# The centre tap of the FFN's convolution, made by GpSimd instead of ScalarE

## The chip, the cores and the metric

One core of one Trainium2 chip runs the whole program in one launch. The metric is the device time of a launch in microseconds. The kernel before takes 1537.39 us, the median of 3 runs (1535.62 to 1537.73).

The core's engines work side by side, each through its own queue in program order, and wait for each other on semaphores: TensorE (PE in the profile; its weight loads are PEld), VectorE (DVE), ScalarE (ACT), GpSimd (POOL), and SyncE (SP), which here issues the DMAs.

## The reference

`x` is [64, 128, 256], `ctx` is [64, 128, 192], all float32. Everything is per sequence of 128 tokens.

```python
# cross attention, 16 heads of 64; the last 4 context tokens have weights and a softmax of their own
xn  = layernorm(x)
q   = xn @ Wq + xn @ q_down @ q_up * (q_alpha / 32)
k,v = the same from ctx[:, :124] with Wk, Wv;   k2,v2 = ctx[:, 124:] @ Wk_ipa, @ Wv_ipa
o   = softmax(q k^T / 8) v + softmax(q k2^T / 8) v2
x   = x + o @ Wo + bo + o @ o_down @ o_up * (o_alpha / 32)
# FFN with quantised activations and ternary weights
h   = quant(layernorm(x)) @ ternary(w1).T                     # [64, 128, 1024]
h   = conv_w[:,0]*h[t-1] + conv_w[:,1]*h[t] + conv_w[:,2]*h[t+1] + conv_b   # per channel, along the tokens
h   = silu(h)
x   = x + quant(h) @ ternary(w2).T
```

The change is in the term `conv_w[:,1]*h[t] + conv_b`, the centre tap.

## The kernel before

**Groups and half-steps.** The 64 sequences are 16 groups of four (`GROUPS`, `NB`). A group is worked in 32 half-steps, n = 0 to 31 (`HALVES`), two to a step; a step is one chunk of attention (one sequence, four heads). Each engine has a function `steps(g, n)` that issues, for half-step n, its part of attention for group g, of the projections for group g+1, and of the FFN (`finish`) for group g-1, whose own half-steps run from 0 to 44 and so reach into g-2's place. `run_groups` (L134) writes this out for groups 0, 1, the last and the two drains, and has a hardware loop for groups 2 to 14. So attention of one group, the projections of the next and the FFN of the one before run beside each other; only the last group's FFN runs alone.

**The FFN's hidden channels** are 8 tiles of 128 channels (`CT`), each 128 partitions by 512 tokens (four sequences of 128). Per tile j, with lags in half-steps:

- TensorE makes the product into one PSUM bank (L591; L543 in the last group, with five banks).
- VectorE multiplies it by the token's scale into `GB[j % 4]` (L1062; L952 in the last group) and signals `g_done`.
- ScalarE makes the centre tap (L777), `HT[j] = CW[:, j, 1] * GB + CB`, and signals `t1_done`. It is at half-steps `M_F1 + M_LAG[0] + M_TILE[j]`, that is 16, 17, 18, 20, 21, 22, 24, 25.
- VectorE adds the tap of the token before (`conv_before`, L1003, after `t1_done`), then the tap of the token after (`conv_next`, L997).
- ScalarE takes tanh of half of it into `GB` (L782), VectorE gates: `HT = (GB + 1) * HT` (L1009). L997, L1003 and L1009 read two tensors from SBUF; L1062 reads one from PSUM and one from SBUF.

`HT[j]` is a view of `HP` in which two tiles are interleaved, so that its elements are two apart. The first four tiles wait besides for the DMA that writes out the group before (`out_done`), since the output lies in the same memory.

**Beside it, per step of attention:** TensorE makes the scores (L500), VectorE the maxima (L913, L914) and the shifted scores of the four extra tokens (L916), ScalarE the exponentials (L751, L754), VectorE sums and reciprocals (L906, L908). GpSimd multiplies the probabilities by the reciprocals (L1238, two instructions), TensorE transposes them in the next step (L487), ScalarE copies (L737), TensorE multiplies with V (L478), ScalarE copies the result twice (L743, L745), GpSimd takes the low part of the split (L1269, signal `ot_done`), and TensorE projects (L513). L745 of a chunk waits for L1269 of the chunk before, because `OF` has one buffer. ScalarE further copies the projections (L718, L719, L724, L730).

**GpSimd's queue** in a half-step is in this order: `project` (L1221, and L1228, which copies extra columns of K), `finish` (L1244, a power of four elements), `residual` (L1276, at n = 16, 18, 20, 22: adds the bias to the residual input), `attend` (L1238, even n), `attend_low` (L1269, odd n). In the hardware loop a function `carrier` puts a one-element instruction ahead of L1228 (L1216).

Of the kernel before, what the change touches and what calls it, by code (L numbers as in the profile page):

```python
# [23 lines left out]
ALU = mybir.AluOpType  # L24
ACT = mybir.ActivationFunctionType
# [12 lines left out]
NB = 4  # L38
# [6 lines left out]
CT = HID // P  # L45
# [26 lines left out]
M_F1 = 15  # L72
M_TILE = (0, 1, 2, 4, 5, 6, 8, 9)
M_LAG = (1, 1, 2, 3, 3)
# [38 lines left out]
def is_last(g):  # L113

    return g.reg is None and g.off == GROUPS - 1
# [7 lines left out]
def tile_at(n):  # L123
    return M_TILE.index(n) if n in M_TILE else -1


def need(eng, sem, value):

    if isinstance(value, int) and value <= 0:
        return  # L130
    eng.wait_ge(sem, value)
# [15 lines left out]
def program(nc, x, ctxT, cipaT, Wq, Wk, Wv, Wo, bo, q_downT, q_up, k_downT, k_up, v_downT, v_up, o_downT, o_up,  # L147
            alphas, Wk_ipa, Wv_ipa, w1T, conv_w, conv_b, w2T, out):
    with ExitStack() as ctx:
        def sb(name, shape, dt=F32):  # L150
            return ctx.enter_context(nc.sbuf_tensor(name, shape, dt))

        def sem(name):
            return ctx.enter_context(nc.semaphore(name))
# [11 lines left out]
        CW = sb("CW", [P, CT, 3])  # L166
        CB = sb("CB", [P, CT])
# [4 lines left out]
        HALF = sb("HALF", [P, NB])  # L172
# [26 lines left out]
        GB = [GBS[:, i] for i in range(4)]  # L199
# [9 lines left out]
        SMALL = sb("SMALL", [P, 8])  # L209
        IDLE = sb("IDLE", [P, 2 + QUADS])  # L210


        HT = [HP[:, j // 2, :, j % 2] for j in range(CT)]
# [58 lines left out]
        f1_full, g_done, t1_done, t2_done, t3_done, th_done, h_done = (  # L272
            sem(n) for n in ("f1_full", "g_done", "t1_done", "t2_done", "t3_done", "th_done", "h_done"))
# [5 lines left out]
        out_done = sem("out_done")  # L279
# [422 lines left out]
        def _(act):  # L702
# [53 lines left out]
            def finish(g, n):  # L756
                if n == L_QT and is_last(g):
                    act.wait_ge(bc_full, g.count(2, 1))
                    need(act, g_done, g.count(CT, 0))
                    act.activation(BC[:], last_bc, ACT.Identity).then_inc(bc_done, 1)  # L760
                if n == M_QT + 1:
                    act.wait_ge(q1t_full, g.count(1, 1))
                    bank = last_q1t if is_last(g) else psF
                    act.activation(Q1T[:].rearrange("p k t -> p (k t)"), bank.bitcast(BF16), ACT.Identity).then_inc(q1t_done, 1)
                if n == M_COPY:
                    act.wait_ge(q2_done, g.count(CT, NB))
                    act.activation(OUTT, X2[:], ACT.Identity).then_inc(copy_done, 1)
                if n == M_BC1 + 1 and not is_last(g):
                    act.wait_ge(bc_full, g.count(2, 1))
                    need(act, g_done, g.count(CT, 0))  # L770
                    act.activation(BC[:], psF, ACT.Identity).then_inc(bc_done, 1)
                j = tile_at(n - M_F1 - M_LAG[0])
                if 0 <= j < CT:
                    act.wait_ge(g_done, g.count(CT, j + 1))
                    if j < NB:
                        need(act, out_done, g.count(16, 0))
                    act.activation(HT[j].rearrange("p (b t) -> p b t", b=NB), GB[j % 4], ACT.Identity,  # L777
                                   bias=CB[:, j:j + 1], scale=CW[:, j, 1:2]).then_inc(t1_done, 1)
                j = tile_at(n - M_F1 - M_LAG[3])
                if 0 <= j < CT:  # L780
                    act.wait_ge(t3_done, g.count(CT, j + 1))
                    act.activation(GB[j % 4], HT[j].rearrange("p (b t) -> p b t", b=NB), ACT.Tanh,  # L782
                                   scale=0.5).then_inc(th_done, 1)
# [416 lines left out]
        @block.gpsimd  # L1200
        def _(pool):
            pool.memset(IDF[:], 0.0).then_inc(ident, 1)
            pool.wait_ge(ident, 1)
            pool.affine_select(out=IDF[:], in_=IDF[:], compare_op=ALU.not_equal, fill=1.0, base=0,
                               pattern=[[-1, P]], channel_multiplier=1).then_inc(ident, 1)
            pool.wait_ge(ident, 2)
            pool.tensor_copy(IDB[:], IDF[:]).then_inc(ident, 1)
            pool.memset(x2_flat, 0.0).then_inc(padded, 1)
            pool.memset(qm_flat[:, 6144:8192], 0.0).then_inc(padded, 1)
            pool.memset(kt_flat[:, 2048:4096], 0.0).then_inc(padded, 1)  # L1210
            pool.wait_ge(consts, 1)

            def carrier(g, i):

                if g.reg is not None:
                    pool.tensor_tensor(IDLE[:, 2 + i:3 + i], HALF[:, 0:1], HALF[:, 0:1], ALU.add)  # L1216

            def project(g, n):
                if n == N_POW:
                    pool.wait_ge(ln1_var, g.count(1, 1))  # L1220
                    pool.tensor_tensor(RS[0][:], VE[0][:], HALF[:], ALU.pow).then_inc(ln1_rstd, 1)  # L1221
                q = quad_at(n - N_V[0])
                if q is not None:
                    pool.wait_ge(ki_in, g.count(16, 16))
                    need(pool, s_full, g.count(CHUNKS, 4 * q + NB - CHUNKS))
                    carrier(g, q)
                    for a in range(2 * q, 2 * q + 2):
                        m = pool.tensor_copy(KT[:, a, :, ORG:TOK], KI[:, a, :].rearrange("p (b j) -> p b j", b=NB))  # L1228
                    m.then_inc(kipa_in, 1)

            def attend(g, n):
                s, half = divmod(n, 2)
                gc, c = chunk_at(g, s - 1)
                if half == 0 and gc.exists():
                    pool.wait_ge(rec_done, gc.count(CHUNKS, c + 1))
                    for i, part in enumerate((SM[c % 2][:, :, 0:ORG], SM[c % 2][:, :, ORG:TOK])):
                        shape = [P, 4, (ORG, IPA)[i]]
                        m = pool.tensor_tensor(part, part, RC[c % 2][:, 4 * i:4 * i + 4].unsqueeze(2).broadcast_to(shape), ALU.mult)  # L1238
                    m.then_inc(p_done, 1)

            def finish(g, n):
                if n == M_POW:
                    pool.wait_ge(ln2_var, g.count(1, 1))
                    pool.tensor_tensor(RS[1][:], VE[1][:], HALF[:], ALU.pow).then_inc(ln2_rstd, 1)  # L1244

            for n in range(EARLY_HALVES):
                project(At(0), n)

            for i in (3, 5):
                raw, high, lo_, _ = splits[i]  # L1250
                pool.wait_ge(w_high, i + 1)
                pool.tensor_tensor(lo_, raw, high.bitcast(F32), ALU.subtract).then_inc(wv_low, 1)
            pool.wait_ge(w_low, 4)
            pool.wait_ge(wv_low, 2)
            pool.wait_ge(du_used, DU_O)
            pool.memset(QM[0:64, :, 1, :], 0.0).then_inc(zeroed, 1)
            pool.wait_ge(zeroed, 1)
            pool.memset(QM[64:128, :, 0, :], 0.0).then_inc(zeroed, 1)
            pool.wait_ge(zeroed, 2)
            pool.wait_ge(du_used, DU_N)  # L1260
            for n in range(EARLY_HALVES, HALVES):
                project(At(0), n)

            def attend_low(g, n):
                s, half = divmod(n, 2)
                gc, c = chunk_at(g, s - 3)
                if half == 1 and gc.exists():
                    pool.wait_ge(ot_high, gc.count(CHUNKS, c + 1))
                    pool.tensor_tensor(OT[1][c % 2][:], OF[:], OT[0][c % 2][:].bitcast(F32),  # L1269
                                       ALU.subtract).then_inc(ot_done, 1)  # L1270

            def residual(g, n):
                if n in (16, 18, 20, 22) and g.exists():
                    b = (n - 16) // 2
                    pool.wait_ge(xres_in, g.count(16, 16))
                    pool.tensor_tensor(XRES[:, b, :], XRES[:, b, :], BO[:], ALU.add).then_inc(xres_done, 1)  # L1276

            def steps(g, n):
                if g.exists():
                    project(g, n + HALVES)  # L1280
                if g.shift(-2).exists():
                    finish(g.shift(-2), n + HALVES)
                if g.shift(1).exists(1):
                    project(g.shift(1), n)
                if g.shift(-1).exists():
                    finish(g.shift(-1), n)
                residual(g, n)
                attend(g, n)
                attend_low(g, n)

            run_groups(pool, steps)
# [32 lines left out]
```

## Time and profile before

| | |
|---|---|
| median of 3 runs | 1537.39 us (1535.62 to 1537.73) |
| the profiled execution | 1535.5 us |
| its span, first to last instruction | 1533.5 us |
| mean granted TensorE clock in it | 0.983 |
| HBM read, written | 36.13 MB, 10.49 MB |

The profile is one execution. Busy time is the time in which an engine has an instruction at work; an instruction's record also holds time in which it stands and waits for something inside the engine or for memory. Records of successive instructions on one engine overlap by some tenths of a microsecond, so what an instruction takes from its queue is better read from the start of one to the start of the next. Spans on GpSimd are rough. "Idle before" is the time in which an engine stood still ahead of an instruction, and who ended it.

### The profile page before, as it was taken

To read this page: it belongs to the slowest core of one execution; us is meant where nothing else is said; L and a number is where in the kernel's file an instruction comes from. 1 tells how busy PE (TensorE), PEld (TensorE's weight loads), DVE (VectorE), ACT (ScalarE), POOL (GpSimd) and SP (SyncE) were. 2 spreads that over 40 slices of the span, in tenths; PEclk is the share of its full clock that TensorE was granted. 3 is DMA by queue.
4 is the path that set the end of the run, shared out by engine and by line. 5 is a ranking of instruction groups with operands and counts; after the bars stand their busy time and mean duration, and the time that the engine had idled before them with its cause. 6 is when DMAs were issued, how large, how long until landed. Compare 5 with 4: busy or idle time off the path is not lost.

```text
span 1533.5 us, 33070 instructions
## 1 busy us (share of the span) xinstructions
PE 1409.5 (92%) x10604; PEld 1159.5 (76%) x10650; DVE 1195.5 (78%) x3059; ACT 1182.3 (77%) x3909; POOL 668.1 (44%) x1058
## 2 busy tenths in 40 slices
PE   7899999999999999999999999999999999999762
PEld 4688778787777878777787878788787777878541
DVE  4363698787969878796887878688787878788888
ACT  3477787978878797887879788787978788797832
POOL 2354444445444444544544454444445444444420
PEclk9999999999999999999999999999999999999985
DMA  9210100000010100000010000001000000100000
GB/s 279 53 31 16 31 16 28 20 28 30 24 34 15 33 11 28 30 28 29 15 44 1 29 28 28 29 15 44 8 23 28 28 29 15 44 1 1 29 15 14
DMA packets 41144, 47.13 MB, mean 31 GB/s; under 512 B 3024, under 2 KB 35216, under 8 KB 41104
## 3 DMA queue, kind: packets, MB, share of 16 engines
q1 hardware_dynamic: 41104, 46.62, 10.1%
q8 instruction: 22, 0.36, 0.1%
q14 instruction: 18, 0.15, 0.0%
HBM read 36.13 MB, written 10.49 MB: 30 GB/s over the span
## 4 chain that ended last, share of the span: by engine, by line
PE 43%; DVE 30%; ACT 17%; issue 9%; DMA 1%; DVEq 0%; POOL 0%; SPq 0%; POOLq 0%; ACTq 0%
PE PS L500 10%; ACT SM L751 8%; PE PS L462 6%; PE PS L443 5%; PE PS L513 5%; PE PS L478 4%; PE PS L487 4%; PE PS L452 3%; PE PS L591 2%; DVE HP L1003 2%; DVE GBS L1062 2%; DVE MX L914 2%; DVE GBS L1086 2%; DVE HP L1009 2%; ACT QM L719 2%
## 5 line engine op out<-in xcount | busy, mean ns | idle before, releaser
L1238 POOL TENSOR_TENSOR SM<-SM,RC 128x496 f32<-128x496 f32 (+1 forms) x512 | 324.2, 654 | 738.6 <-DVE RC L908 738.6
L751 ACT ACTIVATE SM<-PS,MX 128x124 f32<-128x124 f32 x1024 | 359.9, 367 | 159.1 <-DVE SM L916 155.8
L500 PE MATMUL PS<-KT,QM 128*128 128x128 f32 x2048 | 278.1, 279 | 24.0 <-ACT SM L751 24.0
L500 PEld LDWEIGHTS PS<-KT,QM 128*128 128x128 f32 x2048 | 249.4, 192 | 38.6 <-ACT SM L751 38.1
L751 ACT ACTIVATION_READ_ACCUMULATOR SM<-PS,MX 128x1 f32 x1024 | 212.2, 207 | 0.0
L1269 POOL TENSOR_TENSOR OTl<-OF,OTh 128x256 fp32r<-128x256 f32 x256 | 204.1, 797 | 10.4 <-ACT OF L745 10.4
L487 PE MATMUL PS<-IDF,SM 128*128 128x128 f32 x1024 | 168.4, 287 | 16.6 <-POOL SM L1238 16.5
L743 ACT ACTIVATE OTh<-PS 128x256 fp32r<-128x256 f32 x256 | 100.4, 392 | 93.5 <-PE PS L478 92.5
L914 DVE TENSOR_REDUCE MX<-PS 128x4 f32<-128x496 f32 x256 | 170.5, 666 | 0.4 <-issue 0.4
L478 PEld LDWEIGHTS PS<-PT,V 128*64 128x64 f32 x2048 | 106.6, 136 | 82.3 <-issue 75.4
L478 PE MATMUL PS<-PT,V 128*64 128x128 f32 x2048 | 168.6, 286 | 0.0
L737 ACT ACTIVATE PT<-PS 128x512 f32<-128x512 f32 x256 | 157.4, 615 | 0.3 <-PE PS L487 0.3
L487 PEld LDWEIGHTS PS<-IDF,SM 128*128 128x128 f32 x1024 | 107.8, 141 | 63.1 <-issue 35.3
L1062 DVE TENSOR_TENSOR GBS<-PS,BC 128x512 f32<-128x512 f32 x120 | 82.5, 688 | 89.6 <-PE PS L591 88.6
L1009 DVE SCALAR_TENSOR_TENSOR HP<-GBS,HP 128x512 f32<-128x512 f32 x128 | 111.6, 872 | 22.0 <-ACT GBS L782 21.0
L513 PE MATMUL PS<-WOh,OTh 128*128 128x256 f32 x512 | 123.5, 322 | 0.7 <-POOL OTl L1269 0.7
L777 ACT ACTIVATE HP<-GBS,CB,CW 128x512 f32<-128x512 f32 x128 | 112.8, 882 | 10.0 <-DVE GBS L952 5.0
L913 DVE TENSOR_REDUCE MX<-PS 128x4 f32<-128x16 f32 x256 | 40.4, 158 | 100.6 <-PE PS L500 99.0
L997 DVE SCALAR_TENSOR_TENSOR HP<-GBS,CW,HP 128x508 f32<-128x508 f32 x128 | 110.0, 860 | 0.1
L443 PE MATMUL PS<-XTh,WQh 128*128 128x512 f32 x256 | 107.3, 419 | 0.0
L1003 DVE SCALAR_TENSOR_TENSOR HP<-GBS,CW,HP 128x508 f32<-128x508 f32 x128 | 97.3, 760 | 11.8 <-ACT HP L777 11.8
L745 ACT ACTIVATE OF<-PS 128x256 f32<-128x256 f32 x256 | 100.8, 394 | 5.4 <-POOL OTl L1269 5.4
(166 smaller groups left out, 3511.5 us busy)
## 6 DMA issues: line engine op xcount, KB each, us to landing
XIN<-in_x SPq DMA_DIRECT2D x16, 512.0 KB, 3.5
XRES<-in_x SPq DMA_DIRECT2D x16, 512.0 KB, 4.6
out_y<-HP SPq DMA_DIRECT2D x15, 512.0 KB, 3.2
CRAW<-in_ctxT SPq DMA_DIRECT2D x16, 256.0 KB, 2.7
RRAW<-in_ctxT SPq DMA_DIRECT2D x32, 128.0 KB, 2.9
QM<-in_Wq SPq DMA_DIRECT2D x1, 1024.0 KB, 9.1
GBS<-in_Wo SPq DMA_DIRECT2D x1, 1024.0 KB, 14.0
k_ipa_columns<-HP SPq DMA_DIRECT2D x1, 1024.0 KB, 6.5
```

What stands on the lines that cost most here:

```text
L443: m = mm(bank, WQ[w][:, k, P * tile:P * tile + P], XT[xt][:, k, :], start=(i == 0), stop=(i == 5))
L478: m = mm(psO[r:r + DH, h // 2, :], V[:, b, DH * (4 * q + h):DH * (4 * q + h) + DH], PT[:, h, :], start=True, stop=True)
L487: m = pe.transpose(psT[:, h, :], SM[c % 2][:, h, :], IDF[:])
L500: m = mm(psS[:, h, :], QM[:, 2 * q + h // 2, h % 2, TOK * b:TOK * b + TOK], KT[:, 2 * q + h // 2, b, :], start=True, stop=True)
L513: m = mm(psY[b // 2][:, b % 2, :], OT[ot][c % 2][:, a, :], WO[w][:, 2 * q + a, :], start=(q == 0 and i == 0 and b % 2 == 0), stop=(q == QU ...
L737: act.activation(PT[:], psT, ACT.Identity).then_inc(pt_done, 1)
L751: m = act.activation(SM[s % 2][:, h, 0:ORG], psS[:, h, 0:ORG], ACT.Exp, bias=MX[s % 2][:, h:h + 1], accum_out=SU[s % 2][:, h:h + 1])
L914: dve.tensor_reduce(MX[s % 2][:, 0:4], psS[:, :, 0:ORG], AX.X, ALU.max, negate=True)
L1003: dve.scalar_tensor_tensor(out=y[:, :, 1:TOK], in0=GB[j % 4][:, :, 0:TOK - 1], scalar=CW[:, j, 0:1], in1=y[:, :, 1:TOK], op0=ALU.mult, op1 ...
L1009: dve.scalar_tensor_tensor(out=y, in0=GB[j % 4], scalar=1.0, in1=y, op0=ALU.add, op1=ALU.mult).then_inc(h_done, 1)
L1238: m = pool.tensor_tensor(part, part, RC[c % 2][:, 4 * i:4 * i + 4].unsqueeze(2).broadcast_to(shape), ALU.mult)
L1269: pool.tensor_tensor(OT[1][c % 2][:], OF[:], OT[0][c % 2][:].bitcast(F32), ALU.subtract).then_inc(ot_done, 1)
```

## The change

The centre tap leaves ScalarE's `finish` and goes into GpSimd's `finish`, at the same half-steps and with the same waits (`g_done`, and `out_done` for the first four tiles), as one `tensor_scalar` with two per-partition operands. It signals the same semaphore `t1_done`. In the hardware loop a one-element `tensor_tensor` on GpSimd stands between the waits and the tap; `carrier` takes its destination as an argument for that. In GpSimd's order the tap stands after `project` and ahead of `residual`, `attend` and `attend_low` of its half-step. ScalarE's other work and that of all other engines is as before.

```diff
--- before.py
+++ after.py
@@ -769,13 +769,6 @@
                     act.wait_ge(bc_full, g.count(2, 1))
                     need(act, g_done, g.count(CT, 0))
                     act.activation(BC[:], psF, ACT.Identity).then_inc(bc_done, 1)
-                j = tile_at(n - M_F1 - M_LAG[0])
-                if 0 <= j < CT:
-                    act.wait_ge(g_done, g.count(CT, j + 1))
-                    if j < NB:
-                        need(act, out_done, g.count(16, 0))
-                    act.activation(HT[j].rearrange("p (b t) -> p b t", b=NB), GB[j % 4], ACT.Identity,
-                                   bias=CB[:, j:j + 1], scale=CW[:, j, 1:2]).then_inc(t1_done, 1)
                 j = tile_at(n - M_F1 - M_LAG[3])
                 if 0 <= j < CT:
                     act.wait_ge(t3_done, g.count(CT, j + 1))
@@ -1210,10 +1203,10 @@
             pool.memset(kt_flat[:, 2048:4096], 0.0).then_inc(padded, 1)
             pool.wait_ge(consts, 1)
 
-            def carrier(g, i):
+            def carrier(g, to):
 
                 if g.reg is not None:
-                    pool.tensor_tensor(IDLE[:, 2 + i:3 + i], HALF[:, 0:1], HALF[:, 0:1], ALU.add)
+                    pool.tensor_tensor(to, HALF[:, 0:1], HALF[:, 0:1], ALU.add)
 
             def project(g, n):
                 if n == N_POW:
@@ -1223,7 +1216,7 @@
                 if q is not None:
                     pool.wait_ge(ki_in, g.count(16, 16))
                     need(pool, s_full, g.count(CHUNKS, 4 * q + NB - CHUNKS))
-                    carrier(g, q)
+                    carrier(g, IDLE[:, 2 + q:3 + q])
                     for a in range(2 * q, 2 * q + 2):
                         m = pool.tensor_copy(KT[:, a, :, ORG:TOK], KI[:, a, :].rearrange("p (b j) -> p b j", b=NB))
                     m.then_inc(kipa_in, 1)
@@ -1242,6 +1235,14 @@
                 if n == M_POW:
                     pool.wait_ge(ln2_var, g.count(1, 1))
                     pool.tensor_tensor(RS[1][:], VE[1][:], HALF[:], ALU.pow).then_inc(ln2_rstd, 1)
+                j = tile_at(n - M_F1 - M_LAG[0])
+                if 0 <= j < CT:
+                    pool.wait_ge(g_done, g.count(CT, j + 1))
+                    if j < NB:
+                        need(pool, out_done, g.count(16, 0))
+                    carrier(g, SMALL[:, j:j + 1])
+                    pool.tensor_scalar(HT[j].rearrange("p (b t) -> p b t", b=NB), GB[j % 4], CW[:, j, 1:2], CB[:, j:j + 1],
+                                       ALU.mult, ALU.add).then_inc(t1_done, 1)
 
             for n in range(EARLY_HALVES):
                 project(At(0), n)
```

## Rows read from the trace of the kernel before

**Rows 1.** The page: busy us, share of the span and instructions of each engine.
```profile
PE 1409.5 (92%) x10604; PEld 1159.5 (76%) x10650; DVE 1195.5 (78%) x3059; ACT 1182.3 (77%) x3909; POOL 668.1 (44%) x1058
```

**Rows 2.** Stretches (columns: length, then the engines named in the first line).
```profile
core 0: us, PE busy (x) PEld busy (x) DVE busy (x) ACT busy (x) POOL busy (x), PEclk, DMA share, GB/s
726.00:756.00 30.00, 28.74 (x216) 23.43 (x215) 27.02 (x56) 28.37 (x87) 14.86 (x23) 1.00 0.04 12
740.80:754.20 13.40, 12.21 (x93) 9.47 (x92) 11.85 (x23) 13.27 (x45) 5.68 (x10) 1.00 0.00 1
1493.20:1512.90 19.70, 1.81 (x7) 0.43 (x5) 19.40 (x30) 10.77 (x15) 0.00 (x0) 0.59 0.00 0
```

**Rows 3.** The chain of waits in one group, by time: start, us, what.
```profile
734.72 0.49 DVE GBS L1062
...
740.81 0.07 ACT SM L751
...
754.19 1.16 PE PS L500 x8
```

**Rows 4.** Instructions in order of time: start us, us, engine, line, operation, tiles.
```profile
737.49 0.43 ACT L745 ACTIVATE OF<-PS 128x256 f32<-128x256 f32 x1
...
738.12 0.37 PE L513 MATMUL PS<-WOh,OTh 128*128 128x256 f32 x1
...
748.94 0.91 ACT L777 ACTIVATE HP<-GBS,CB,CW 128x512 f32<-128x512 f32 x1
...
749.67 0.43 ACT L743 ACTIVATE OTh<-PS 128x256 fp32r<-128x256 f32 x1
...
751.51 0.16 DVE L916 TENSOR_TENSOR SM<-PS,MX 128x16 f32<-128x16 f32 x1
...
752.64 0.36 ACT L751 ACTIVATE SM<-PS,MX 128x124 f32<-128x124 f32 x1
```

**Rows 5.** Groups by line and shape: count, busy us, mean ns, idle before.
```profile
L777 ACT ACTIVATE HP<-GBS,CB,CW 128x512 f32<-128x512 f32 x128 | 112.8, 882 | 10.0 <-DVE GBS L952 5.0 <-DMA out_y<-HP 3.5
...
L1009 DVE SCALAR_TENSOR_TENSOR HP<-GBS,HP 128x512 f32<-128x512 f32 x128 | 111.6, 872 | 22.0 <-ACT GBS L782 21.0
...
L997 DVE SCALAR_TENSOR_TENSOR HP<-GBS,CW,HP 128x508 f32<-128x508 f32 x128 | 110.0, 860 | 0.1
...
L1003 DVE SCALAR_TENSOR_TENSOR HP<-GBS,CW,HP 128x508 f32<-128x508 f32 x128 | 97.3, 760 | 11.8 <-ACT HP L777 11.8
...
L1062 DVE TENSOR_TENSOR GBS<-PS,BC 128x512 f32<-128x512 f32 x120 | 82.5, 688 | 89.6 <-PE PS L591 88.6
...
L1238 POOL TENSOR_TENSOR SM<-SM,RC 128x496 f32<-128x496 f32 x256 | 259.5, 1014 | 738.6 <-DVE RC L908 738.6
...
L1252 POOL TENSOR_TENSOR WVRl<-QM,WVRh 128x1024 fp32r<-128x1024 f32 x1 | 3.1, 3067 | 1.4 <-ACT WVRh L789 1.4
...
L1209 POOL MEMSET QM<- 128x2048 f32 x1 | 1.8, 1804 | 0.0
```

**Rows 6.** VectorE (DVE) and GpSimd (POOL) instructions in order of time, same columns.
```profile
218.48 1.26 DVE L1009 SCALAR_TENSOR_TENSOR HP<-GBS,HP 128x512 f32<-128x512 f32 x1
...
219.13 0.66 POOL L1228 COPY KT<-RRAW 128x16 f32<-128x16 f32 x1
...
729.60 0.74 DVE L1003 SCALAR_TENSOR_TENSOR HP<-GBS,CW,HP 128x508 f32<-128x508 f32 x1
...
729.72 1.22 POOL L1269 TENSOR_TENSOR OTl<-OF,OTh 128x256 fp32r<-128x256 f32 x1
...
730.26 1.23 DVE L1009 SCALAR_TENSOR_TENSOR HP<-GBS,HP 128x512 f32<-128x512 f32 x1
...
735.42 1.24 POOL L1269 TENSOR_TENSOR OTl<-OF,OTh 128x256 fp32r<-128x256 f32 x1
```

**Rows 7.** Single lines over the span: duration in ns, min/median/max.
```profile
L1269 POOL TENSOR_TENSOR OTl<-OF,OTh x256: 721/736/1269, 87.1 to 1473.2; 128x256 fp32r<-128x256 f32 x128
...
L1009 DVE SCALAR_TENSOR_TENSOR HP<-GBS,HP x128: 676/692/1259, 195.6 to 1512.2; 128x512 f32<-128x512 f32 x128
```

## The prediction

> **What bounds the kernel now.** I read the page's busy shares first: TensorE is busy 92% of the span, VectorE and ScalarE 78% and 77%, GpSimd 44% [rows 1]. Averages over a kernel with stages decide nothing, so I went to the stretch in which the convolution runs. It comes once per group of four sequences, 15 times beside attention, and a sixteenth time alone at the end. In one such group it is the stretch from 719 to 757 us. Its dense part, 726 to 756, has VectorE busy 27.02 of 30.00 us, ScalarE 28.37, TensorE 28.74, and GpSimd only 14.86 [rows 2]. Three engines are full at once, and none has more than 2.98 us to give.
>
> Which of them ends last inside the stretch is in the chain of waits [rows 3]: TensorE up to 734.7, then VectorE's convolution up to 740.8, then ScalarE to 754.2, where TensorE takes over. From 740.8 to 754.2 ScalarE is busy 13.27 of 13.40 us [rows 2]. So ScalarE is a real bound, for 13 us of a group, and VectorE is close behind it: VectorE hands over the maxima (L916) at 751.51 + 0.16 = 751.67, and the exponentials that need them start at 752.64, only 0.97 us later [rows 4].
>
> **The change, part by part.**
>
> *Removed from ScalarE:* 128 centre taps (L777) of 0.882 us by their records [rows 5]. The record of the next instruction starts before the end of the last, so the queue is freed by 749.67 - 748.94 = 0.73 us for each [rows 4], 8 x 0.73 = 5.8 us per group. Only two taps (745.7 and 748.9) stand in the part that ScalarE bounds, so at most 2 x 0.73 = 1.46 us per group could come off the path, and after 0.97 us VectorE's maxima are late next. 15 groups: 15 to 22 us gained, if nothing else moved.
>
> *Added to GpSimd:* 128 instructions of 512 elements with one tensor input, and for the 13 groups in the loop (104 taps) a one-element instruction ahead of each. The trace has no such tap. From below: a memset of 2048 elements takes 1.804 us, which scaled to 512 is 0.45 us. From above: a two-input subtraction of 1024 elements takes 3.067 us, scaled 1.53 us. The nearest row is the normalisation of 496 elements, two inputs, 1.014 us [rows 5]. I take 0.95 us, an estimate, and keep 0.45 and 1.53 for the range. GpSimd has the time: 8 x 0.95 = 7.6 us plus 8 x 0.2 us for the small ones against 15.1 idle in the 30. So it is not a question of GpSimd's load, but of whom the tap meets.
>
> *Whom it meets.* VectorE's taps and gate (L997, L1003, L1009) read two tensors from SBUF, and the trace shows what GpSimd does to them. L1003 starts at 729.60 and ends at 730.34; GpSimd's L1269, which starts at 729.72 and mostly takes 0.74 (its median [rows 7]), ends at 730.94, just 0.60 after it. L1009 starts at 730.26, while L1269 is at work, and ends at 731.49, 0.55 after L1269: 1.23 us [rows 6] in place of a median of 0.69 [rows 7]. They take turns, whole instructions at a time, the first come first. The mean of L1009, 0.872, holds such waits. L1062, which reads PSUM and SBUF, has a mean of 0.688 [rows 5] and is not stretched. That an instruction on GpSimd with one input stands in the same line shows at 219.13: a copy of 16 elements takes 0.66 us, to 219.79, beside an L1009 that ends at 219.74 [rows 6].
>
> The Trainium skill (SBUF — State Buffer, "Who interferes with whom") has the same as a rule: a VectorE instruction with two SBUF inputs contends with a GpSimd instruction that reads SBUF, for the whole instruction. It covers a one-input tap. The trace agrees as far as its rows go (1.23 us in place of 0.69 above), but has no VectorE instruction that waits behind a long one-input one. By this rule the change costs what I work out next; without it, the second rival's time.
>
> A tap is released at the end of L1062, and VectorE starts its next instruction at once. Taking the order of the code: tap 0 is followed by attention's small reductions and meets nothing. Tap 1 waits for L1003, runs under the next L1062 (0.60 us that need no turn), and holds the next L997 for the rest, 0.2 us. Taps 2 to 7 each wait for the two-input instruction that has just begun and then hold the next of them: 0.95 - 0.14 (the lead in, 0.74 - 0.60 from L1269) - 0.1 (queued ahead) = 0.7 us. Sum 6 x 0.7 + 0.2 = 4.4 us more on VectorE per group. Its idle time in the dense part, 2.98 us, swallows the first part; 4.4 - 3.0 = 1.4 us per group remain. ScalarE's relief doesn't get this back, since its exponentials now wait for VectorE.
>
> *Moved on GpSimd:* the tap's wait stands ahead of the residual addition (L1276), the normalisation (L1238) and the low part (L1269), in program order. Worst is tap 4. Today L1269 ends at 735.42 + 1.24 = 736.66, and ScalarE's L745 needs it at 737.49, TensorE's L513 at 738.12 [rows 4, 6]. The tap in front, with the turns that it waits for, takes about 0.8 to 2 us, so that both may stall 0.5 to 1 us, in the stretch where VectorE is late anyway. The normalisation is wanted by TensorE only in the next step of some 5.8 us and has 2 us of slack. I put these stalls beside VectorE's delay, not on top of it; on top, they would be another 0.5 us per group, 8 us.
>
> *Nothing for DMA:* no transfer changes; the last group's tap 0 waits for the output of the group before either way.
>
> *The last group,* alone: VectorE is busy 19.40 of 19.70 us from 1493.2 to 1512.9 [rows 2], and GpSimd has nothing else. The same 4.4 us less 0.3 of idle: 4 us.
>
> **Sum.** 15 x 1.4 + 4 = 25 us. The profiled execution took 1535.5 us (span 1533.5), so 1560.5; the median of the runs shown is 1537.39, 1.9 above it: 1562 us.
>
> **The rivals.**
>
> *A long tap.* At the upper bound of 1.53 us each tap holds VectorE for 1.3 us: 6 x 1.3 + 0.8 = 8.6, less 3.0 = 5.6 us per group, 84 + 8 = 92 us, 1629. Half way, a tap of 1.2 us: 6 x 0.95 + 0.5 - 3.0 = 3.2 per group, 55 us with the end, 1592. For it: two multipliers taken from pointers, and an output in steps of two elements (a tile's rows lie interleaved in HP), which no GpSimd row shows. Against it: 1.014 us for nearly as many elements with two inputs.
>
> *ScalarE's relief wins: faster.* Place: 740.8 to 754.2. If a one-input tap takes no turn, or is as short as a memset (0.45 us, hold 0.2 us, 6 x 0.2 = 1.2 us, inside the 2.98 of idle), VectorE keeps its times and ScalarE gives back 0.97 to 1.46 us per group: 15 to 22 us, 1515 to 1522; I put it at 1520. It decides where the hold is below about 0.5 us a tap. Against it: 0.45 us is an instruction that reads nothing, and the one-input copy that had to wait at 219.13.
>
> *A draw.* The hold of 0.5 us fills the idle time and ScalarE's relief pays for the rest: 1537, within 3 us. It needs both to meet closely.
>
> **How the numbers follow.** Forecast 0.50 (1546 to 1580 by itself), long tap 0.18, faster 0.20, draw 0.12. The measurement tells a difference of about 0.2%, 3 us, from no change. Slower by more holds the forecast and the long tap, 0.68; within it lies the draw, 0.12; faster 0.20. The range has to reach into both sides: down to 1526, which leaves out most of the faster case's lower part, up to 1600, which leaves out the long tap's upper half.
>
> **What would show it.** Right: L777's place taken by a GpSimd group of 128 with about 0.95 us where it runs alone, and longer, up to 1.6, where it waits; the means of L997, L1003 and L1009 up from 0.860, 0.760 and 0.872 [rows 5] by 0.2 us or so on average (4.4 us over the 24 of a group), L1062's unchanged; ScalarE's wait for L916 grown; the distance from group to group up by 1.4 us; the last group longer by 4 us. Wrong: means of VectorE's taps as before with taps on GpSimd running beside them (the turn is not taken), a tap far from 0.95 us, or a chain that leads through L1269 and L745 in the stretch, which would make the queue order and not the turn the cause.

## The result and the profile after

The changed kernel takes 1573.57 us (1572.62 to 1574.94, 4 runs) against 1536.86 us: a ratio of 1.0241, interval 1.0226 to 1.0256. It is 36.7 us slower; 25 were forecast. The forecast's side and range hold. Its size was a third too small, and the way in which the loss comes about was only half seen.

Lines have moved up by 7 in the middle of the program: L996 after is L1003 before, L990 is L997, L1002 is L1009, L1055 is L1062, L907 and L909 are L914 and L916, L775 is L782, L945 is L952, L1231 is L1238, L1270 is L1269, L1277 is L1276. The tap is L1244, the one-element instruction L1209. In the written-out kernels below (e7, e10) the same lines stand 3 higher up, so that the tap's place is L1241.

The page after, first the engines' busy us, then the shares of the chain that ended last, that is, of the chain of waits that leads back from the last instruction:

```profile
PE 1422.5 (90%) x10604; PEld 1165.9 (74%) x10650; DVE 1229.3 (78%) x3059; ACT 1097.5 (70%) x3781; POOL 884.6 (56%) x1290
...
PE 31%; DVE 25%; POOL 22%; issue 11%; ACT 10%; DMA 1%; DVEq 0%; POOLq 0%; SPq 0%; ACTq 0%
```

The same chain before:

```profile
PE 43%; DVE 30%; ACT 17%; issue 9%; DMA 1%; DVEq 0%; POOL 0%; SPq 0%; POOLq 0%; ACTq 0%
```

GpSimd had no share in the chain before; now it has 22%, and ScalarE has fallen from 17% to 10%. The engine that was given work became part of the bound, though it is busy only 56% of the span [rows 1: 44% before].

The groups by line and shape, same columns as [rows 5]:

```profile
L1244 POOL TENSOR_SCALAR HP<-GBS,CW,CB 128x512 f32<-128x512 f32 x128 | 150.3, 1175 | 31.3 <-DVE GBS L1055 14.4 <-DMA out_y<-HP 11.1 <-DVE GBS L945 5.2
L996 DVE SCALAR_TENSOR_TENSOR HP<-GBS,CW,HP 128x508 f32<-128x508 f32 x128 | 135.6, 1059 | 16.4 <-POOL HP L1244 16.3
...
L990 DVE SCALAR_TENSOR_TENSOR HP<-GBS,CW,HP 128x508 f32<-128x508 f32 x128 | 117.8, 921 | 0.1
...
L1002 DVE SCALAR_TENSOR_TENSOR HP<-GBS,HP 128x512 f32<-128x512 f32 x128 | 101.0, 789 | 26.2 <-ACT GBS L775 26.1
L745 ACT ACTIVATE OF<-PS 128x256 f32<-128x256 f32 x256 | 99.3, 388 | 82.8 <-POOL OTl L1270 82.8
...
L1055 DVE TENSOR_TENSOR GBS<-PS,BC 128x512 f32<-128x512 f32 x120 | 82.3, 685 | 84.0 <-PE PS L591 82.4
...
L1209 POOL TENSOR_TENSOR SMALL<-HALF 128x1 f32<-128x1 f32 x104 | 54.1, 520 | 95.9 <-DVE GBS L1055 93.1
```

The tap and the 104 new one-element instructions over the span, min/median/max in ns:

```profile
L1244 POOL TENSOR_SCALAR HP<-GBS,CW,CB x128: 797/1248/1884, 186.0 to 1546.7; 128x512 f32<-128x512 f32 x128
```
```profile
L1209 POOL TENSOR_TENSOR SMALL<-HALF x104: 186/628/642, 276.7 to 1403.2; 128x1 f32<-128x1 f32 x104
```

And the wait for the low part, before:

```profile
ACT OF L745 <- POOL OTl L1269: 5.4, 14, 0.4
```

A tap alone takes 0.797 us; its mean is 1.175, so on average 0.38 us of it is standing. The 128 records fall into three lots: 56 of 0.80 to 0.82 us, 45 of 1.24 to 1.32, and 27 of 1.74 to 1.88. The one-element instructions take 0.520 us on average for 0.19 of work: 78 of the 104 took 0.63 us. VectorE's three two-input instructions go from 318.9 us in total [rows 5: 111.6 + 110.0 + 97.3] to 354.4, 2.2 us more per group. That is 0.09 us for each instruction where 0.2 was forecast, and it isn't spread evenly: L996 is longer by 0.30 us on average, L990 by 0.06, and L1002 is shorter by 0.08. L1055, which reads PSUM, stays at 0.685. A new wait stands out: ScalarE's copy L745 stood still for 82.8 us before GpSimd's low part L1270 was done. It was 5.4 us before. Not all of that is loss, since ScalarE has been relieved of 112.8 us of taps.

Where this happens I read from the stretch of the convolution, from the start of a group's first product (L591) to the start of its first channel maximum (L1005, L1012 before). In a group of the loop these are, before and then after:

```profile
719.52 0.38 PE L591 MATMUL PS<-Q1T,W 128*128 128x512 bf16 x1 [0.79 <-ACT BC L771]
```
```profile
756.96 1.21 DVE L1012 TENSOR_REDUCE GBS<-HP 128x128 f32<-128x1024 f32 x1
```
```profile
824.46 0.38 PE L591 MATMUL PS<-Q1T,W 128*128 128x512 bf16 x1 [0.76 <-ACT BC L771]
```
```profile
864.38 1.21 DVE L1005 TENSOR_REDUCE GBS<-HP 128x128 f32<-128x1024 f32 x1
```

Before it is 756.96 - 719.52 = 37.4 us, after 864.38 - 824.46 = 39.9. The same reading of all 16 groups, here and in the experiments below, gives this table (us; "between" is from one stretch's end to the next one's start, mean of 13; "last group" is from its first L1003 to its first maximum):

| kernel | group 0 | groups 1 to 13, mean | group 14 | last group | between |
|---|---|---|---|---|---|
| before | 37.86 | 37.46 | 33.73 | 19.68 | 51.57 |
| after | 39.09 | 39.94 | 38.30 | 21.04 | 51.55 |
| e1, tap last in its half-step | 40.68 | 41.78 | 38.84 | 21.05 | 52.07 |
| e2, fill without a read | 37.20 | 38.89 | 33.42 | 19.70 | 51.34 |
| e4, ScalarE's tap short | 37.15 | 36.77 | 35.56 | 19.68 | 51.34 |
| e5, GpSimd's tap short | 37.44 | 38.65 | 33.90 | 19.94 | 51.34 |
| e9, two small ones | 39.30 | 40.96 | 38.20 | 21.03 | 51.35 |
| e6, before without loop | 38.12 | 38.09 | 33.97 | 19.68 | 51.31 |
| e7, after without loop | 39.31 | 39.31 | 38.39 | 21.04 | 51.31 |
| e10, fill, without loop | 37.22 | 37.09 | 33.54 | 19.71 | 51.32 |

All of the loss lies in the stretch: 1.23 + 13 x 2.48 + 4.57 + 1.36 = 39.4 us, and the spans differ by 1572.5 - 1533.5 = 39.0. (The traces before and after have 51.6 us between the stretches, nearly all others 51.3, so a row of e2 and below differs from the first two by some 3 us in total that the stretches don't show.) Groups 1 to 13 have their FFN in the hardware loop and so have one-element instructions ahead of the taps; group 0, group 14 and the last have none. Group 14 runs with no projections beside it.

How a stretch grows is best seen at tile 7 of one group. First VectorE, then GpSimd, then ScalarE, in order of time:

```profile
763.30 0.69 DVE L1002 SCALAR_TENSOR_TENSOR HP<-GBS,HP 128x512 f32<-128x512 f32 x1
763.90 0.75 DVE L990 SCALAR_TENSOR_TENSOR HP<-GBS,CW,HP 128x508 f32<-128x508 f32 x1
765.21 1.19 DVE L996 SCALAR_TENSOR_TENSOR HP<-GBS,CW,HP 128x508 f32<-128x508 f32 x1 [0.55 <-POOL HP L1244]
```
```profile
762.81 0.63 POOL L1209 TENSOR_TENSOR SMALL<-HALF 128x1 f32<-128x1 f32 x1
763.42 1.75 POOL L1244 TENSOR_SCALAR HP<-GBS,CW,CB 128x512 f32<-128x512 f32 x1
765.13 0.72 POOL L1270 TENSOR_TENSOR OTl<-OF,OTh 128x256 fp32r<-128x256 f32 x1
```
```profile
765.89 0.38 ACT L745 ACTIVATE OF<-PS 128x256 f32<-128x256 f32 x1 [1.48 <-POOL OTl L1270]
```

The one-element instruction's record runs from 762.81 to 763.44. The tap behind it starts at 763.42, but L1002 and L990 follow each other without a gap on VectorE, and the tap gets its turn after both: L990 ends at 764.65, the tap at 765.17, 1.75 us for 0.8. Meanwhile L996 of this tile waits for the tap, 0.55 us. Then GpSimd's low part L1270 goes ahead of it, and L996 takes 1.19 us in place of 0.74. And L1270, whose input an L745 had written by 759.88, comes so late that the next L745, which writes the same buffer, stands for 1.48 us. So one tap delays VectorE and ScalarE together, and the delay goes through GpSimd's queue.

That queue is full in the middle of the stretch. GpSimd is busy 32.5 of its 39.9 us (824.46 to 864.38), where it was busy 18.1 of 37.5 before. In the group shown above its records follow each other without a gap from 738.54 to 758.44:

```profile
757.22 1.22 POOL L1270 TENSOR_TENSOR OTl<-OF,OTh 128x256 fp32r<-128x256 f32 x1
759.67 0.63 POOL L1209 TENSOR_TENSOR SMALL<-HALF 128x1 f32<-128x1 f32 x1 [1.23 <-DVE GBS L1055]
```

The chain of waits stays on GpSimd in this group from 734.2 to 765.9 and leaves it by the low part for ScalarE's copy (here with the pieces between left out):

```profile
743.17 2.04 POOL SM L1231 x2
745.22 1.14 POOL OTl L1270
...
765.17 0.69 POOL OTl L1270
765.89 0.04 ACT OF L745
```

The chain gives GpSimd a little too much, as it counts to it the 1.23 us before 759.67, in which it waits for VectorE. The records without a gap show the full queue without the chain's help.

### The profile page after: what moved, and what is told of

It reads as the page before. It is cut to its first block, busy times and chain, and to the rows that moved or that the text cites. A ratio compares the mean times of both kernels' runs of the same rounds, so it can differ in the third digit from the quotient of the medians.

```text
span 1572.5 us, 33265 instructions
## 1 busy us (share of the span) xinstructions
PE 1422.5 (90%) x10604; PEld 1165.9 (74%) x10650; DVE 1229.3 (78%) x3059; ACT 1097.5 (70%) x3781; POOL 884.6 (56%) x1290
## 4 chain that ended last, share of the span: by engine, by line
PE 31%; DVE 25%; POOL 22%; issue 11%; ACT 10%; DMA 1%; DVEq 0%; POOLq 0%; SPq 0%; ACTq 0%
PE PS L500 7%; POOL SM L1231 6%; POOL HP L1244 5%; ACT SM L751 5%; PE PS L462 5%; POOL OTl L1270 4%; PE PS L443 4%; PE PS L513 3%; POOL SMALL L1209 3%; PE PS L487 3%; POOL XRES L1277 3%; PE PS L478 2%; DVE GBS L1079 2%; PE PS L452 2%; PE PS L612 2%
## 5 line engine op out<-in xcount | busy, mean ns | idle before, releaser
L1231 POOL TENSOR_TENSOR SM<-SM,RC 128x496 f32<-128x496 f32 (+1 forms) x512 | 344.3, 693 | 469.2 <-DVE RC L901 469.2
L1270 POOL TENSOR_TENSOR OTl<-OF,OTh 128x256 fp32r<-128x256 f32 x256 | 209.4, 818 | 10.4 <-ACT OF L745 10.4
L743 ACT ACTIVATE OTh<-PS 128x256 fp32r<-128x256 f32 x256 | 99.2, 388 | 112.8 <-PE PS L478 111.6
L907 DVE TENSOR_REDUCE MX<-PS 128x4 f32<-128x496 f32 x256 | 170.3, 665 | 0.4 <-issue 0.4
L1244 POOL TENSOR_SCALAR HP<-GBS,CW,CB 128x512 f32<-128x512 f32 x128 | 150.3, 1175 | 31.3 <-DVE GBS L1055 14.4
L745 ACT ACTIVATE OF<-PS 128x256 f32<-128x256 f32 x256 | 99.3, 388 | 82.8 <-POOL OTl L1270 82.8
L487 PEld LDWEIGHTS PS<-IDF,SM 128*128 128x128 f32 x1024 | 108.2, 141 | 60.5 <-issue 33.1
L996 DVE SCALAR_TENSOR_TENSOR HP<-GBS,CW,HP 128x508 f32<-128x508 f32 x128 | 135.6, 1059 | 16.4 <-POOL HP L1244 16.3
L1055 DVE TENSOR_TENSOR GBS<-PS,BC 128x512 f32<-128x512 f32 x120 | 82.3, 685 | 84.0 <-PE PS L591 82.4
L1002 DVE SCALAR_TENSOR_TENSOR HP<-GBS,HP 128x512 f32<-128x512 f32 x128 | 101.0, 789 | 26.2 <-ACT GBS L775 26.1
L990 DVE SCALAR_TENSOR_TENSOR HP<-GBS,CW,HP 128x508 f32<-128x508 f32 x128 | 117.8, 921 | 0.1
L1209 POOL TENSOR_TENSOR SMALL<-HALF 128x1 f32<-128x1 f32 x104 | 54.1, 520 | 95.9 <-DVE GBS L1055 93.1
```

Source lines behind the costliest of these rows:

```text
L487: m = pe.transpose(psT[:, h, :], SM[c % 2][:, h, :], IDF[:])
L907: dve.tensor_reduce(MX[s % 2][:, 0:4], psS[:, :, 0:ORG], AX.X, ALU.max, negate=True)
L990: dve.scalar_tensor_tensor(out=y[:, :, 0:TOK - 1], in0=GB[j % 4][:, :, 1:TOK], scalar=CW[:, j, 2:3], in1=y[:, :, 0:TOK - 1], op0=ALU.mult, ...
L996: dve.scalar_tensor_tensor(out=y[:, :, 1:TOK], in0=GB[j % 4][:, :, 0:TOK - 1], scalar=CW[:, j, 0:1], in1=y[:, :, 1:TOK], op0=ALU.mult, op1 ...
L1244: pool.tensor_scalar(HT[j].rearrange("p (b t) -> p b t", b=NB), GB[j % 4], CW[:, j, 1:2], CB[:, j:j + 1], ALU.mult, ALU.add).then_inc(t1_d ...
```

## The experiments

Two theories were set against each other. *Turn:* the loss is there because the tap reads SBUF, for which it and VectorE's two-input instructions take turns. *Queue:* it is there because the tap, its wait and its length stand ahead of other work in GpSimd's order. All medians are beside runs of the kernel before on the same chip, whose medians were 1536.2 to 1537.3. e2 and e10 leave the tap's value out and e4 and e5 most of it; they stand here for their times alone.

**e1_tap_last.** GpSimd's tap goes behind the rest of its half-step.

```diff
+            def tap(g, n):
                 j = tile_at(n - M_F1 - M_LAG[0])
 ...
                 attend_low(g, n)
+                if g.shift(-2).exists():
+                    tap(g.shift(-2), n + HALVES)
+                if g.shift(-1).exists():
+                    tap(g.shift(-1), n)
```

> The changed kernel, with GpSimd's tap moved behind the residual addition, the normalisation and the low part of its own half-step, instead of ahead of them. The same instructions run, and the same ones read SBUF. Queue theory (the 37 us come from what stands behind the tap in GpSimd's queue): most of it comes back, 1540 to 1550 us, and the waits of L745 and L513 for the low part fall to the 5 and 1 us of the kernel before. Turn theory (the 37 us come from VectorE's two-input instructions, which wait while a tap reads): little changes, 1565 to 1575 us.

Measured: 1608.70 us, ratio 1.0474 (1.0456 to 1.0491), 35 us slower than the changed kernel. Both theories missed. VectorE's wait for the tap, and ScalarE's for the low part:

```profile
DVE HP L996 <- POOL HP L1246: 73.3, 87, 2.0
...
ACT OF L745 <- POOL OTl L1272: 23.4, 29, 1.4
```

L745's wait falls from 82.8 to 23.4 us, as the queue theory said, but L996 now waits 73.3 us for the tap in place of 16.3. The tap ties VectorE's convolution to attention's work on the same queue, whichever goes first. In this order it costs more, and GpSimd keeps its 22% of the chain.

**e2_no_read.** The tap becomes a fill of the same tile, which reads nothing.

```diff
-                    pool.tensor_scalar(HT[j]..., GB[j % 4], CW[:, j, 1:2], CB[:, j:j + 1], ALU.mult, ALU.add)
+                    pool.memset(HP[:].bitcast(BF16)[:, j // 2, :, 2 * (j % 2):2 * (j % 2) + 2], 0.5)
```

> The changed kernel, with the tap replaced by a fill of the same tile, written as 1024 half-width elements so that it takes about as long (0.8 to 0.9 us) but reads nothing from SBUF. The tap's value is left out. Its place, its waits and the one-element instruction ahead of it stay. Turn theory: a fill that reads nothing doesn't hold VectorE's two-input instructions, so their means fall to those of before (0.87, 0.76, 0.86 us) and the time to 1540 to 1550 us. Queue theory: GpSimd's queue is as long as before, 1565 to 1575 us.

Measured: 1550.61 us, ratio 1.0091 (1.0074 to 1.0108), 23 us faster than the changed kernel, 0.6 above the turn theory's range. The table shows more than the median: in the three groups that have no one-element instruction, the loss is gone altogether (37.20, 33.42, 19.70 against 37.86, 33.73, 19.68). In the loop 1.4 us per group stay, and the kernel is still 14.3 us slower than the kernel before: GpSimd has 20% of its chain, and ScalarE waits 56.5 us for the low part. VectorE's means didn't fall as far as expected: L996 is at 0.990. Two kinds of reading instruction are left that could hold it, the one-element instructions and the low part.

**e4_act_short.** ScalarE's relief alone, in the kernel before.

```diff
-  act.activation(HT[j].rearrange("p (b t) -> p b t", b=NB), GB[j % 4], ...
+  act.activation(HT[j].rearrange("p (b t) -> p b t", b=NB)[:, :, 0:1], GB[j % 4][:, :, 0:1], ...
```

> The kernel before, with ScalarE's tap cut to one token per sequence (4 elements of 512; the rest of the tap is left out), so that ScalarE is relieved and GpSimd gets nothing. This is what the relief alone is worth. The prediction's bound: 15 to 22 us less than before, 1515 to 1522 us. If VectorE is the bound through the whole stretch: no more than 5 us less, 1532 or above.

Measured: 1523.09 us, ratio 0.9911 (0.9894 to 0.9927): 13 us, 1 us short of the bound's range. The relief is real, 0.7 us per group of the loop, less than the 0.97 us by which VectorE's maxima were behind [rows 4]. Group 14 became 1.8 us longer in its stretch; why was not followed up.

**e5_tap_short.** GpSimd's tap cut in the same way, to 4 elements.

```diff
-  pool.tensor_scalar(HT[j].rearrange("p (b t) -> p b t", b=NB), GB[j % 4], ...
+  pool.tensor_scalar(HT[j].rearrange("p (b t) -> p b t", b=NB)[:, :, 0:1], GB[j % 4][:, :, 0:1], ...
```

> The changed kernel, with GpSimd's tap cut to one token per sequence (4 elements of 512; the rest is left out). The waits ahead of the residual addition, the normalisation and the low part stay, as does the one-element instruction; the 0.8 us of work go. If the length of the tap makes the loss, in the queue or in turns, the time falls below that of the kernel before, to 1520 to 1535 us. If the waits in GpSimd's order (the tap's input comes late, and what is behind it waits) make it, 1555 or above.

Measured: 1548.43 us, ratio 1.0079 (1.0063 to 1.0096), between both ranges. The short tap is not free:

```profile
L1244 POOL TENSOR_SCALAR HP<-GBS,CW,CB 128x4 f32<-128x4 f32 x128 | 99.6, 778 | 36.4 <-DVE GBS L1055 17.4 <-DMA out_y<-HP 11.6 <-DVE GBS L945 7.3
```
```profile
L1244 POOL TENSOR_SCALAR HP<-GBS,CW,CB x128: 344/792/1957, 186.2 to 1520.1; 128x4 f32<-128x4 f32 x128
```

Its 4 elements take 0.778 us on average, 0.344 at the least: it reads, so it stands in line. This didn't isolate the length.

**e6_before_no_loop, e7_after_no_loop.** The loop over groups written out in both kernels, so that the one-element instructions go.

```diff
-    with eng.Fori(2, GROUPS - 1) as reg:
-        for n in range(HALVES):
-            steps(At(0, reg, 2, GROUPS - 2), n)
-    for g in (GROUPS - 1, GROUPS, GROUPS + 1):
+    for g in range(2, GROUPS + 2):
```

> The kernel before, with the hardware loop over groups 2 to 14 written out, so that no wait stands against a register and GpSimd needs no one-element instruction ahead of a wait (52 fewer). Base for the next run. Expected 1533 to 1540 us: nothing else changes.

> The changed kernel, with the hardware loop written out: the 104 one-element instructions ahead of the taps go, the taps stay. In the trace of the changed kernel the FFN stretch of group 0, which has no one-element instructions, is 1.2 us longer than before, those of the loop 2.5. If the one-element instructions make the other half (they read SBUF, so they take turns with VectorE too), this run is 23 us above the written-out kernel before (13 x 1.23 + 4.57 + 1.36 us). If they are free, it is 37 us above.

Measured: 1539.72 us, ratio 1.0020 (1.0011 to 1.0030), and 1561.82 us, ratio 1.0156 (1.0139 to 1.0173). They are 22.1 us apart, where 23 were expected. Per group of the loop the taps cost 39.31 - 38.09 = 1.22 us without the small ones, 2.48 with them. So the difference between loop and written-out form makes about 13 x 1.26 = 16 of the 37 us, read across two bases, as writing out costs the kernel before 3.6 us by itself. Read from the two changed kernels alone it is 1573.57 - 1561.82 = 11.8 us. Writing out removes the loop's waits against a register together with the one-element instructions, so neither figure is the price of these instructions by themselves; e9 adds such instructions and nothing else. Without one ahead of it the tap waits itself: its mean is 1.417 us in e7, against 1.175 and 0.520 in the loop.

**e9_two_small.** The small instruction doubled.

```diff
                     carrier(g, SMALL[:, j:j + 1])
+                    carrier(g, SMALL[:, (j + 4) % 8:(j + 4) % 8 + 1])
```

> The changed kernel, with a second one-element instruction ahead of each of the 104 taps in the loop. It has next to no work (0.13 us from start to start) but reads SBUF. Turn theory: it stands 0.6 us in line like the first, so GpSimd's queue is 8 x 0.5 us longer per group and the time grows by 10 to 25 us, to 1583 to 1598. If only the work of an instruction counts: 13 x 8 x 0.13 = 14 us at the most and mostly hidden, 1574 to 1580.

Measured: 1584.50 us, ratio 1.0310 (1.0293 to 1.0327), 10.9 us more. That is the low end of the turn theory's range. Each of these reads of one element costs 0.1 us of the kernel's time. The 104 added ones took 87.2 - 54.1 = 33.1 us together, 0.32 each, and the taps behind them waited less (mean 1.038 in place of 1.175). The second pays the 0.63 us again in 39 cases of 104, and the loop's stretch grows by 40.96 - 39.94 = 1.02 us, which is also about 8 x 0.13, the bare time taken in the expectation (0.14 from start to start in this trace). So this run doesn't tell the two readings apart as sharply as I had meant it to.

```profile
L1245 POOL TENSOR_SCALAR HP<-GBS,CW,CB 128x512 f32<-128x512 f32 x128 | 132.9, 1038 | 31.3 <-DVE GBS L1055 14.5 <-DMA out_y<-HP 11.1 <-DVE GBS L945 5.2
...
L1209 POOL TENSOR_TENSOR SMALL<-HALF 128x1 f32<-128x1 f32 x208 | 87.2, 441 | 84.4 <-DVE GBS L1055 82.3
```

**e10_no_read_no_loop.** e2's fill and e7's written-out loop together, the deciding run.

> The written-out changed kernel, with the tap replaced by the fill that reads nothing (the tap's value is left out). No one-element instruction, no read: what stays of the change is ScalarE's relief, and the tap's wait and length in GpSimd's queue. Turn theory: reading alone made the loss, so this is faster than the written-out kernel before by ScalarE's relief, 0.65 us for each of 15 groups, 1528 to 1532 us against its 1539.7. Queue theory (wait and length in GpSimd's order cost by themselves): 1545 us or above.

Measured: 1520.82 us, ratio 0.9891 (0.9874 to 0.9907). By the medians it is 18.9 us faster than the written-out kernel before and 41.0 faster than the written-out changed kernel, from which it differs only in the 128 instructions that don't read: a fill in place of a multiply and add. (The profiled execution, from which the table's row is, is the slowest of its four, 1525.4 us; by the profiled spans the two differences are 14.3 and 37.4.) The time is 7 us below the range that the turn theory had given, and more than e4's 13 us below its base; what makes the rest is open. The fill is longer than a tap, waits for the same, and stands in the same place:

```profile
L1241 POOL MEMSET HP<- x128: 947/954/966, 187.5 to 1498.4; 128x1024 bf16 x128
```

The chain of this kernel:

```profile
PE 46%; DVE 33%; ACT 11%; POOL 6%; issue 3%; DMA 1%; SPq 0%; DVEq 0%; POOLq 0%
```

947 to 966 ns: never held, though 100 of the 128 fills start while one of VectorE's two-input instructions is at work. From the start of a fill to the start of the next instruction, where that follows directly, it is 0.89 to 0.92 us throughout. The queue theory by itself is out: with the same order, the same wait and a longer instruction, but no read and no small instruction, nothing is lost and ScalarE's relief comes through. What is lost in the changed kernel needs the turns. They make it in large part by filling GpSimd's queue, and e2, with 20% of its chain on GpSimd, shows that with the small instructions and the loop this costs time even when the tap itself takes no turn.

**e8_two_taps, e13_two_taps_no_loop.** Only tiles 6 and 7 on GpSimd, with a semaphore of their own (`t1_gp`); tiles 0 to 5 on ScalarE. e13 has the loop written out besides.

```diff
+GP = 6
 ...
-                if 0 <= j < CT:      # GpSimd
+                if GP <= j < CT:
 ...
+                if 0 <= j < GP:      # ScalarE, the tap as before the change
```

> The changed kernel, with only the taps of tiles 6 and 7 on GpSimd; those of tiles 0 to 5 are back on ScalarE. These two are the taps in the part that ScalarE bounds, and GpSimd is idle just ahead of them. If the relief there outweighs the turns of two taps: 1527 to 1533 us, a gain on the kernel before. If a tap costs VectorE 0.3 us or more wherever it stands: 1538 to 1545 us.

> The written-out kernel with only the taps of tiles 6 and 7 on GpSimd. Against the written-out kernel before (1539.7). If the one-element instructions made the 6.5 us that the two-tap kernel with the loop lost: 1533 to 1539 us, the relief wins. If the turns of the two taps themselves make it: 1541 to 1546 us.

Measured: 1542.69 us, ratio 1.0038 (1.0024 to 1.0052), and 1545.64 us, ratio 1.0051 (1.0034 to 1.0067): 6.5 and 5.9 us above their bases, both in the range given for a tap that costs more than it relieves. Even two taps in ScalarE's own stretch don't pay, with or without small ones. They wait longest of all, 1.571 us on average in e8 and longer in e13:

```profile
L1251 POOL TENSOR_SCALAR HP<-GBS,CW,CB 128x512 f32<-128x512 f32 x32 | 62.2, 1944 | 65.2 <-DVE GBS L1064 42.1 <-DVE GBS L951 23.1
```

1.944 us for 0.8. No tap of e13 runs without a wait: 22 take 1.74 to 1.86 us and 10 take 2.34 or 2.35, where in the one at 303.35 VectorE runs through L1005, L1011 and L996 first, each starting before the last has ended.

**e11_after_late_residual, e12_before_late_residual.** The four residual additions (L1276) moved out of the convolution's stretch, in both kernels.

```diff
-                if n in (16, 18, 20, 22) and g.exists():
-                    b = (n - 16) // 2
+                if n in (28, 29, 30, 31) and g.exists():
+                    b = n - 28
```

> The changed kernel, with the four residual additions of a group on GpSimd moved from half-steps 16, 18, 20, 22 (among the taps) to 28 to 31 (behind the last tap, beside reductions of one input on VectorE). They take 3 us of GpSimd's queue and read SBUF. Turn and queue both let the convolution's stretch shorten: 5 to 15 us faster than the changed kernel, 1558 to 1569 us. If GpSimd has time enough in the stretch and only the taps matter: 1572 to 1575.

> The kernel before, with the same four residual additions moved to half-steps 28 to 31. In its trace only some of them meet two-input instructions on VectorE. If they hold VectorE at all: 1 to 6 us faster than before, 1530 to 1535. If they only wait themselves: 1535 to 1538, no change.

Measured: 1563.84 us, ratio 1.0172 (1.0155 to 1.0189), 9.7 us better than the changed kernel; and 1535.71 us, ratio 0.9991 (0.9981 to 1.0001), no change. GpSimd's queue has slack in the stretch of the kernel before; in the changed one, what is taken off it comes back in part, 0.44 us in a group of the loop (39.94 to 39.50) and 3.2 us in group 14 (38.30 to 35.13). No version that computes the whole tap beats the kernel before by more than its measurement tells.

## Why the prediction was right in its side and short in its size

- *What bounds the kernel.* Right for the kernel before. ScalarE's relief is worth 13.2 us (e4), a little under the 15 to 22 given as a bound.
- *The tap's length,* 0.95 us taken, is 0.797 alone. The Trainium skill (GPSIMD Engine Reference, "Performance versus the Vector engine") has 769 ns for 512 elements of a tight loop; the trace agrees, with 797 ns for its shortest tap. The long tap is out as a rival.
- *The turn.* Right: e10 against e7, 41 us by the medians, for 128 instructions that read against 128 that don't. The Trainium skill's rule (SBUF — State Buffer, "Who interferes with whom") says that an instruction that only writes is exempt; e10's fill, 947 to 966 ns throughout, agrees.
- *The sum on VectorE* was mis-sized: 4.4 us more per group forecast, 2.2 measured. I let VectorE do the waiting. More often the tap does: its mean is 0.38 us above its length and that of the one-element instructions 0.33 us above theirs, 8 x 0.7 = 5.7 us per group on GpSimd's queue.
- *GpSimd's load and the stalls through the low part* are the step that failed. The text had "So it is not a question of GpSimd's load, but of whom the tap meets", and of the stalls "I put these stalls beside VectorE's delay, not on top of it"; on top they would be 0.5 us per group. It is a question of both: with what its instructions wait, GpSimd has no gap for 19.9 us of a stretch, and the chain leads through it for 22% of the span. A chain through L1269 and L745 was named as what would show the prediction wrong in its cause, and it is there (765.17, 765.89 above). It is half wrong: the queue carries the delay, but without the turn it has none to carry (e10). L745's wait of 82.8 us is no measure of the loss: in e7 it is 63.7, and e10, which loses nothing, still has 23.4.
- *The one-element instructions* were given 0.2 us each of GpSimd's idle time and no price. They took 0.520. Loop and small instructions together made 12 to 16 of the 37 us (e7 against the changed kernel, and against e6), and 104 more of them cost 10.9 (e9).
- *The idle time* of 2.98 us on VectorE that was to swallow the first part: 2.48 us were lost per group of the loop where 1.4 were forecast, more than VectorE's own growth of 2.2. In group 14, which has no projections and no small instructions, 4.57 us were lost. That this is near the undiscounted 4.4 is chance, as VectorE's 24 two-input instructions grew by only 1.1 us there (20.82 to 21.91). The chain runs over GpSimd there:

```profile
1474.06 1.76 POOL HP L1244
...
1482.39 2.04 POOL SM L1231 x2
1484.48 0.87 PE PS L487 x4
```

- *The size without the small instructions.* e7 is 22.1 us above e6, close to the 25 of the sum. Its parts don't fit so well: 1.22 us per group of the loop where 1.4 were forecast, 4.4 in group 14 for 1.4, and 1.36 in the last for 4. The last two errors nearly cancel, which is luck.
- *The last group:* 4 us forecast, 1.36 measured. There is no other work on GpSimd to delay, and six of its eight taps wait through two of VectorE's instructions (1.75 to 1.88 us) rather than hold the second:

```profile
1532.19 0.74 DVE L990 SCALAR_TENSOR_TENSOR HP<-GBS,CW,HP 128x508 f32<-128x508 f32 x1
1532.85 0.74 DVE L996 SCALAR_TENSOR_TENSOR HP<-GBS,CW,HP 128x508 f32<-128x508 f32 x1
1533.62 1.08 DVE L990 SCALAR_TENSOR_TENSOR HP<-GBS,CW,HP 128x508 f32<-128x508 f32 x1
```
```profile
1532.37 1.80 POOL L1244 TENSOR_SCALAR HP<-GBS,CW,CB 128x512 f32<-128x512 f32 x1 [0.19 <-DVE GBS L945]
```

- *The faster rival* was to need only a tap that takes no turn, and was put at 1520 us. For the kernel as changed, e2 is that case, and it takes 1550.6 us: the small instructions in the loop would have kept it slower than before all the same. Only e10, which has none, gets to 1520.8, from a base of 1539.7.

What stays open: how much of the 12 to 16 us between loop and written-out form is the one-element instructions' own turn, how much the position that it gives the tap, and how much the loop's waits. A small instruction that only writes, in their place, would tell; it was not tried.

## What to carry to other kernels

Before work moves to an engine with idle time, ask what it will share there. A GpSimd instruction that reads SBUF beside VectorE instructions with two SBUF inputs costs both, and what stands behind it in GpSimd's queue pays as well; here 13 us of relief turned into 37 us of loss on an engine 44% busy. So add up the queue of the new engine in that stretch with its waits, not only its work. Of the work tried here, only one that only writes came through, and only without small reading instructions ahead of it. Count these too: one element took 0.63 us beside VectorE's instructions and 0.19 alone.

## What was not expected of the hardware

The turn is not always given to the one that came first, as the prediction had it. GpSimd's L1269, queued at 729.72 during L1003, got in ahead of L1009 [rows 6]; the tap queued at 1532.37, during L990, had to let L996 pass as well, though L996 started 0.48 us later. It is no rare case. Of the changed kernel's 128 taps 27 took 1.74 to 1.88 us, as long as the two shown that let two instructions pass (1.75 and 1.80); in e7 it is 67, and in e13 ten taps took 2.34 us or more, of which the one looked at (303.35) let three pass. What decides between getting in and being passed was not separated.
